# An adaptive feed-forward layer on one core: conditioning weights asked for ahead of x, and one x load and its maxima moved in the step before the second half

## The chip, the cores and the metric

The kernel runs on one core of one Trainium2 chip. Its metric is device time in microseconds, the lower the better. The kernel before was timed in three runs: 1572.83, 1573.0 and 1580.12 us, a median of 1573.0 us.

## The reference, cut to what matters

```python
x: (32, 128, 2048) f32       # batch, channel, time
w = weights[itok]            # one of 32 matrices (128 x 128) for each batch entry
c = einsum('bct,bcd->bdt', x, w)                       # conditioning
result = einsum('bnd,od->bno', c, W_base) + b_base     # W_base 2048 x 2048
logits = einsum('bnd,ed->bne', c, W_gate)              # 8 experts
route_w = top-2 of softmax(logits), normalised, as a one-hot sum
h = einsum('bnd,erd->bner', c, A)                      # rank 16 for each expert
delta = einsum('bner,eor->bno', h * route_w[..., None], B)
out = x + result + delta * SCALING
```

## The kernel before, in words

**Tiling.** The 32 batch entries go in 16 pairs. The contraction over 2048 time steps is cut into two halves of 1024. A step `n` (0 to 31, `NSTEP`) is one pair and one half: `pair(n)` gives pair `n % 16` and half `n // 16`. Steps 0 to 15 (`NP` is 16) use the first half of W_base, and store partial sums in `part_scratch`; steps 16 to 31 load these partial sums, add the second half and the low-rank delta, and store `out`. Float32 values are split into two float16 parts and scaled by powers of two, which is why the largest values of x and of the chosen conditioning matrix must be found before anything else is done with them.

**One step on TensorE.** `product(n, s, q)` (L1485) multiplies in a seven-product scheme (q from 0 to 6), for the two column halves `s`; a product is 12 matmuls of 128x512. Between them lie the conditioning of step n+1 (`cond`), `make_features(n)` (L1541, 48 matmuls into bank_h, which reads `FT`), `transpose_maxima(n+1)` (L1530), `spread_maxima(n+1)` (L1536, after product q=2) and in the second half `transpose_hw(n)` (L1574, after q=4). The order in the program is product(n,0,0), make_features(n), transpose_maxima(n+1), product q=1, product q=2, spread_maxima(n+1), q=3, q=4, transpose_hw(n).

**VectorE.** `find_maxima(n)` (L1007) waits for x and for both w_cond tiles, and reduces them: L1011 reads x, L1013 reads w_cond. `finish(n, s, c)` (L1059) turns a finished product into an output tile in `t_sums`: L1070 and L1075. There are eight tiles a step, numbered m = 8n + 4s + c; `t_sums` has two buffers, so tile m waits until GpSimd has added tile m-2. At the end of a step VectorE runs find_maxima(n+2), then finish of C12, C21 and C22 of s = 1. The next step begins with `find_top(n+1)` (L1016), `features(n)` (L1083) and, in the second half, `route_tokens` and `weigh_features` (L1103 to L1150).

**GpSimd.** `add_bias(m)` (L571, L574) waits for the loaded residual tile `x_res` m and adds the bias; `add_r(m)` (L594, L602) adds what `finish` made. In the first half the order is add_bias(m+1), then add_r(m).

**Queues.** SyncE issues nearly all DMAs, in an order written out by hand (L489 on). At j = 0 of a step it stores tile 8n, may store a piece of transformed W_base (`store_piece`, L408), stores h, calls `load_x(n+2)` (L380) once `xp_lo` says that the buffer X has been read, and then loads residual tile m+5. Step 15 has extra loads at j = 0: h0 and `FT`, the second half's feature weights. ScalarE copies product results (`copy_p`, L697) and issues, through its own DMA queue, the 14 loads of 1 MB that replace the weights TT in steps 15 and 16 (`load_weights`, L805, the issue is L812). For s = 1, q = 0 that load waits until the last pieces that store_piece wrote have landed, the last one being the store that step 15 issues just after its tile 120.

Of the kernel before, what the change touches and what calls it, by code (L numbers as in the profile page):

```python
# [9 lines left out]
NP = NB // 2  # L10
KH = T // 2
# [42 lines left out]
def adaln_ffn_kernel(nc, x, idx, w_cond, w_base, b_base, w_gate, a_lora, b_lora, out):  # L54
# [6 lines left out]
    with ExitStack() as ctx:  # L61
# [317 lines left out]
        def _(sp):  # L379
            def load_x(n):  # L380
                p, k = pair(n)
                sp.dma_start(X[:, :, :], x[2 * p:2 * p + 2, :, k * KH:(k + 1) * KH].rearrange("b p t -> p b t")
                             ).then_inc(x_in, 16)
                for i in range(2):
                    b = 2 * p + i
                    row = sp.value_load(idx_sb[0:1, b:b + 1], min_val=0, max_val=w_cond.shape[0] - 1)
                    sp.dma_start(WC[:, i, :], w_cond[bass.ds(row, 1)].rearrange("a c d -> c (a d)")
                                 ).then_inc(wc_in, 16)

            def load_rows(g):  # L390
                k, u = g // NU, g % NU
# [97 lines left out]
            for n in range(NSTEP):  # L489
                p, k = pair(n)  # L490
                g, chunks = window_of(n)
                if chunks:
                    if chunks[0] == 0:
                        store_inv(g)
                    store_piece(g, chunks[0], 0)
                    store_piece(g, chunks[0], 1)
                    store_piece(g, chunks[1], 0)
                    if len(chunks) > 2:
                        store_piece(g, chunks[1], 1)
                for j in range(4 if n == 0 else 0, 8):  # L500
                    m = 8 * n + j
                    store_tile(m)
                    if len(chunks) == 2 and j == 0:
                        store_piece(g, chunks[1], 1)
                    if n == NP - 1 and j == 0:
                        sp.wait_ge(bg_out[H0_PIECE], piece_turn(NU - 1, C4 - 2, 1))
                        sp.wait_ge(h_out, 16)
                        sp.dma_start(h0[:, :, :].rearrange("p b n -> p (b n)"), h_dram[0]).then_inc(h_in, 16)
                        sp.wait_ge(h_done, NP)
                        sp.wait_ge(ft_out, 16)  # L510
                        sp.dma_start(FT[:, :, :, :].rearrange("p f s n -> p (f s n)"), ft_dram).then_inc(ft_in, 16)
                    if len(chunks) > 2 and j == 0:
                        store_piece(g, chunks[2], 0)
                    if j == 0:
                        if k == 0:
                            sp.wait_ge(h_ready, n + 1)
                            sp.dma_start(h_dram[p], h[:, :, :].rearrange("p b n -> p (b n)")).then_inc(h_out, 16)
                        if n + 2 < NSTEP:
                            sp.wait_ge(xp_lo, 2 * (n + 2))
                            load_x(n + 2)  # L520
                        if k == 1 and n + 1 < NSTEP:
                            sp.wait_ge(h_ready, n + 1)
                            sp.dma_start(h0[:, :, :].rearrange("p b n -> p (b n)"), h_dram[p + 1]).then_inc(h_in, 16)
                    if len(chunks) > 2 and j == 0:
                        store_piece(g, chunks[2], 1)
                        store_piece(g, chunks[3], 0)
                    if len(chunks) > 2 and j == 1:
                        store_piece(g, chunks[3], 1)
                    if m > 0 and m - 1 + NXR < 8 * NSTEP:
                        last = m - 1  # L530
                        sp.wait_ge(xr_out[xr_slot(last)], xr_turn(last))
                        load_tile(last + NXR)
                    if n < len(WINDOWS) and j == (4 if n == 0 else 3):
                        sp.wait_ge(cond_done, 4 * (n + 2))
                        load_rows_ahead(*window_ahead(n))
                    if n == NP - 1 and j == 3:
                        sp.wait_ge(bg_inv_out, 16 * NU)
                        load_inv(0)
                    if n == NP - 1 and j == 6:
                        sp.wait_ge(bt_out, 16)  # L540
                        sp.dma_start(BT[:, :, :].rearrange("p s o -> p (s o)"), bt_dram).then_inc(bt_in, 16)
                if n == NP - 1:
                    load_inv(1)
# [451 lines left out]
        def _(dve):  # L995
# [11 lines left out]
            def find_maxima(n):  # L1007
                if n > 0:
                    dve.wait_ge(amax_tr, n)
                dve.wait_ge(x_in, 16 * (n + 1))  # L1010
                nc.vector.tensor_reduce(amax[:, 0:2], X[:, :, :], AX_X, ALU.max, apply_absolute_value=True)  # L1011
                dve.wait_ge(wc_in, 32 * (n + 1))
                nc.vector.tensor_reduce(amax[:, 2:4], WC[:, :, :], AX_X, ALU.max,  # L1013
                                        apply_absolute_value=True).then_inc(amax_ready, 1)
# [330 lines left out]
            for n in range(1, NSTEP):  # L1345
                more, second = n + 1 < NSTEP, n >= NP
                g, chunks = window_of(n)
                whole = len(chunks) > 2
                ahead, ahead_chunks = window_ahead(n)
                if chunks:  # L1350
                    add_up_first(g, chunks[0])
                if n <= NP:
                    find_top(n + 1)
                features(n)
                if n > NP and more:
                    find_top(n + 1)
                if second:
                    route_tokens(n)
                    weigh_features(n)
                if chunks:  # L1360
                    lower_chunk(g, chunks[0])
                finish(n, 0, C11)
                if more:
                    scale_x(n + 1)
                if whole:
                    lower_chunk(g, chunks[1])
                if second:
                    split_hwT_lo(n)
                if more:
                    split_x_lo(n + 1, 0)  # L1370
                    split_x_lo(n + 1, 1)
                if chunks and not whole:
                    lower_chunk(g, chunks[1])
                if whole:
                    lower_chunk(g, chunks[2])
                finish(n, 0, C12)
                if whole:
                    lower_chunk(g, chunks[3])
                if second:
                    add_delta(n, 0)  # L1380
                finish(n, 0, C21)
                finish(n, 0, C22)
                if second and more:
                    s_lower(n + 1, A11)
                if second:
                    add_delta(n, 1)
                if not second:
                    s_lower(n + 1, A11)
                    s_lower(n + 1, S1)
                    sum_s2(n + 1)  # L1390
                    s_lower(n + 1, A12)
                    finish(n, 1, C11)
                    s_lower(n + 1, S2)
                    sum_s4_s3(n + 1)
                    s_lower(n + 1, A22)
                    s_lower(n + 1, S4)
                    s_lower(n + 1, S3)
                else:
                    if more:
                        s_lower(n + 1, S1)  # L1400
                        sum_s2(n + 1)
                    add_delta(n, 2)
                    if more:
                        s_lower(n + 1, A12)
                    finish(n, 1, C11)
                    add_delta(n, 3)
                    if more:
                        s_lower(n + 1, S2)
                        sum_s4_s3(n + 1)
                        s_lower(n + 1, A22)  # L1410
                    add_delta(n, 4)
                    if more:
                        s_lower(n + 1, S4)
                        s_lower(n + 1, S3)
                    add_delta(n, 5)
                if ahead_chunks and ahead_chunks[0] == 0:
                    scales_ahead(ahead)
                if n + 2 < NSTEP:
                    find_maxima(n + 2)
                finish(n, 1, C12)  # L1420
                if second:
                    add_delta(n, 6)
                    add_delta(n, 7)
                finish(n, 1, C21)
                finish(n, 1, C22)
# [317 lines left out]
```

## Time and profile before

| What | Value |
|---|---|
| median of three runs | 1573.0 us (1572.83 to 1580.12) |
| the profiled execution's own time | 1578.86 us |
| its span, first to last instruction | 1577.0 us |
| TensorE (PE) busy | 1511.6 us, 96% |
| VectorE (DVE) busy | 1356.1 us, 86% |
| ScalarE (ACT) busy | 626.0 us, 40% |
| GpSimd (POOL) busy | 647.4 us, 41% |
| mean granted TensorE clock | 0.985 of full speed |
| mean DMA rate over the span | 150 GB/s |

Busy time is the time in which an engine executes; the span is what the engines are shares of. TensorE is busy nearly all the time, so only time in which it is idle, or runs at a lower clock, can be won without removing matmuls. Two stretches of the page's forty show it: the first few, where all engines wait for each other, and the two around the middle of the span, where the DMA rate is at its highest (246, 336 and 225 GB/s in three slices) and VectorE falls from 9 tenths to 6 and 7.

### The profile page before, as it was taken

To read this page: it belongs to the slowest core of one execution; us is meant where nothing else is said; L and a number is where in the kernel's file an instruction comes from. 1 tells how busy PE (TensorE), PEld (TensorE's weight loads), DVE (VectorE), ACT (ScalarE), POOL (GpSimd) and SP (SyncE) were. 2 spreads that over 40 slices of the span, in tenths; PEclk is the share of its full clock that TensorE was granted. 3 is DMA by queue.
4 is the path that set the end of the run, shared out by engine and by line. 5 is a ranking of instruction groups with operands and counts; after the bars stand their busy time and mean duration, and the time that the engine had idled before them with its cause. 6 is when DMAs were issued, how large, how long until landed. Compare 5 with 4: busy or idle time off the path is not lost.

```text
span 1577.0 us, 25816 instructions
## 1 busy us (share of the span) xinstructions
PE 1511.6 (96%) x9411; PEld 812.0 (51%) x9411; DVE 1356.1 (86%) x2257; ACT 626.0 (40%) x1026; POOL 647.4 (41%) x508
## 2 busy tenths in 40 slices
PE   5778999999899999999989999999999999999998
PEld 5554555555455555555535455555455555455553
DVE  5787999999899999999967888888888888888875
ACT  6854454444544445444413332223332323332321
POOL 2564656666666565665622122122122122122122
PEclk8899999999999999999999999999999999999999
DMA  6234556655565555665796343344433344433342
GB/s 232 94 132 150 159 168 179 191 158 157 153 184 170 165 162 178 179 187 153 246 336 225 107 125 100 98 141 128 114 121 96 105 141 123 117 117 91 117 111 74
DMA packets 169567, 235.95 MB, mean 150 GB/s; under 512 B 71898, under 2 KB 88794, under 8 KB 167130
## 3 DMA queue, kind: packets, MB, share of 16 engines
q1 hardware_dynamic: 167426, 219.63, 46.0%
q10 hardware_dynamic: 2016, 14.68, 2.4%
q8 instruction: 75, 1.23, 0.3%
q14 instruction: 50, 0.41, 0.1%
HBM read 147.83 MB, written 86.43 MB: 149 GB/s over the span
## 4 chain that ended last, share of the span: by engine, by line
PE 66%; DVE 17%; issue 4%; DMA 3%; POOL 2%; ACT 1%; SPq 0%; ACTq 0%; DVEq 0%; POOLq 0%
PE bank_x L1429 8%; PE bank_x L1431 8%; PE bank_x L1430 7%; PE bank_y L1429 7%; PE bank_y L1430 7%; PE bank_y L1431 7%; DVE t_sums L1070 3%; PE bank_z L1429 2%; PE bank_z L1431 2%; PE bank_z L1430 2%; DVE t_sums L1075 2%; PE bank_h L1430 2%; PE bank_h L1429 2%; PE bank_h L1431 2%; DVE s_parts L1045 2%
## 5 line engine op out<-in xcount | busy, mean ns | idle before, releaser
L602 POOL TENSOR_TENSOR x_res<-x_res,t_sums 128x512 f32<-128x512 f32 x255 | 353.5, 1388 | 837.6 <-DVE t_sums L1075 676.5
L1429 PE MATMUL bank_y<-TT,s_parts 128*128 128x512 f16 x768 | 294.6, 384 | 4.7 <-DVE TT L1185 4.2
L1430 PE MATMUL bank_y<-TT,s_parts 128*128 128x512 f16 x768 | 294.4, 383 | 0.0
L1431 PE MATMUL bank_y<-TT,s_parts 128*128 128x512 f16 x768 | 294.1, 383 | 0.0
L1429 PE MATMUL bank_x<-TT,s_parts 128*128 128x512 f16 x768 | 291.7, 380 | 1.6 <-DVE TT L1185 1.6
L1430 PE MATMUL bank_x<-TT,s_parts 128*128 128x512 f16 x768 | 291.1, 379 | 0.0
L1431 PE MATMUL bank_x<-TT,s_parts 128*128 128x512 f16 x768 | 291.1, 379 | 0.0
L710 ACT ACTIVATE p_copies<-bank_x,y_inv 128x512 f32<-128x512 f32 x128 | 87.7, 685 | 408.9 <-PE bank_x L1431 298.9
L1075 DVE TENSOR_TENSOR t_sums<-t_sums,inv_w 128x512 f32<-128x512 f32 x255 | 230.7, 905 | 8.7
L1045 DVE TENSOR_TENSOR s_parts<-a_full,s_parts 128x512 f16<-128x512 f32 x224 | 200.0, 909 | 33.6 <-ACT s_parts L695 33.6
L574 POOL TENSOR_TENSOR x_res<-x_res,BT 128x512 f32<-128x512 f32 x128 | 210.7, 1646 | 25.5 <-DMA x_res<-in_x_dram 24.2
L695 ACT ACTIVATE s_parts<-a_full 128x512 f16<-128x512 f32 x224 | 139.0, 628 | 145.8 <-DVE a_full L1050 61.1
L1431 PEld LDWEIGHTS bank_y<-TT,s_parts 128*128 128x128 f16 x768 | 75.9, 99 | 92.8 <-issue 3.9
L1431 PEld LDWEIGHTS bank_x<-TT,s_parts 128*128 128x128 f16 x768 | 75.2, 98 | 90.8 <-issue 0.3
L1429 PEld LDWEIGHTS bank_y<-TT,s_parts 128*128 128x128 f16 x768 | 75.8, 99 | 87.8 <-DVE TT L1185 4.7
L676 ACT ACTIVATE a_full<-bank_c 128x512 f32<-128x512 f32 x128 | 76.2, 595 | 112.6 <-PE bank_c L1431 112.6
L1070 DVE SCALAR_TENSOR_TENSOR t_sums<-bank_y,y_inv,p_copies 128x512 f32<-128x512 f32 x128 | 95.1, 743 | 28.4 <-PE bank_y L1431 28.4
L1429 PEld LDWEIGHTS bank_x<-TT,s_parts 128*128 128x128 f16 x768 | 75.1, 98 | 84.5 <-DVE TT L1185 1.5
L1430 PEld LDWEIGHTS bank_y<-TT,s_parts 128*128 128x128 f16 x768 | 75.8, 99 | 82.9 <-issue 2.8
L1430 PEld LDWEIGHTS bank_x<-TT,s_parts 128*128 128x128 f16 x768 | 75.2, 98 | 82.2 <-issue 0.3
L1070 DVE SCALAR_TENSOR_TENSOR t_sums<-bank_x,y_inv,p_copies 128x512 f32<-128x512 f32 x128 | 95.0, 743 | 10.6 <-PE bank_x L1431 6.7
L1429 PE MATMUL bank_c<-w_cond_parts,x_parts 128*128 128x128 f16 x512 | 93.0, 220 | 4.8 <-ACT a_full L676 2.6
(243 smaller groups left out, 2757.5 us busy)
## 6 DMA issues: line engine op xcount, KB each, us to landing
x<-in_x_dram SPq DMA_DIRECT2D x32, 1024.0 KB, 6.1
x_res<-in_x_dram SPq DMA_DIRECT2D x128, 256.0 KB, 4.2
part_scratch<-x_res SPq DMA_DIRECT2D x128, 256.0 KB, 3.6
x_res<-part_scratch SPq DMA_DIRECT2D x128, 256.0 KB, 3.9
out_dram<-x_res SPq DMA_DIRECT2D x128, 256.0 KB, 2.8
wt_scratch<-late_words SPq DMA_DIRECT2D x64, 224.0 KB, 3.4
TT<-wt_scratch ACTq DMA_DIRECT2D x14, 1024.0 KB, 7.7
x_parts<-in_L_ffn_W_base_dram SPq DMA_DIRECT2D x18, 512.0 KB, 6.6
```

The source lines that it names most:

```text
L574: link(nc.gpsimd.tensor_tensor(XR[:, xr_slot(m), :], XR[:, xr_slot(m), :], bias[:, o:o + Q], ALU.add))
L602: nc.gpsimd.tensor_tensor(XR[:, xr_slot(m), :], XR[:, xr_slot(m), :], TM[:, m % 2, :], ALU.add).then_inc(r_added, 1)
L676: nc.scalar.activation(AF[:, u, :], BC[:, :], ACT.Copy, scale=Y_DOWN).then_inc(af_copied, 1)
L695: nc.scalar.activation(SO[:, slot(n, q), 0, :, :], quads(AF[:, af_of[q], :]), ACT.Copy).then_inc(s_hi, 1)
L710: nc.scalar.activation(PC[:, at, :], src[:, :], ACT.Copy, scale=y_inv[:, par, row:row + 1]).then_inc(p_copied, 1)
L1045: nc.vector.tensor_tensor(SO[:, slot(n, q), 1, :, :], quads(AF[:, af_of[q], :]), SO[:, slot(n, q), 0, :, :], ALU.subtract).then_inc(s_lo, 1)
L1070: nc.vector.scalar_tensor_tensor(out=TM[:, m % 2, :], in0=src[:, :], scalar=y_inv[:, n % 2, c // 2:c // 2 + 1], in1=PC[:, at, :], op0=ALU. ...
L1075: nc.vector.tensor_tensor(TM[:, m % 2, :], TM[:, m % 2, :], inv_w[:, o:o + Q], ALU.mult).then_inc(r_ready, 1)
L1429: nc.tensor.matmul(dst, lhs[0], rhs[0], start=start, stop=False, skip_group_check=chained)
L1430: nc.tensor.matmul(dst, lhs[0], rhs[1], start=False, stop=False, skip_group_check=chained)
L1431: return nc.tensor.matmul(dst, lhs[1], rhs[0], start=False, stop=stop, skip_group_check=chained)
```

## The change

In `load_x` the two loads of w_cond (with the register loads that find their addresses) are issued ahead of the load of x, in all 32 steps. In step 15 alone, `load_x(17)` is issued right behind the store of tile 120, ahead of the weight piece, h0, `FT` and the store of h; and VectorE runs `find_maxima(17)` behind `finish(15, 1, C12)`, no longer ahead of it.

```diff
             def load_x(n):
                 p, k = pair(n)
-                sp.dma_start(X[:, :, :], x[2 * p:2 * p + 2, :, k * KH:(k + 1) * KH].rearrange("b p t -> p b t")
-                             ).then_inc(x_in, 16)
                 for i in range(2):
                     b = 2 * p + i
                     row = sp.value_load(idx_sb[0:1, b:b + 1], min_val=0, max_val=w_cond.shape[0] - 1)
                     sp.dma_start(WC[:, i, :], w_cond[bass.ds(row, 1)].rearrange("a c d -> c (a d)")
                                  ).then_inc(wc_in, 16)
+                sp.dma_start(X[:, :, :], x[2 * p:2 * p + 2, :, k * KH:(k + 1) * KH].rearrange("b p t -> p b t")
+                             ).then_inc(x_in, 16)
@@
                     store_tile(m)
+                    if n == NP - 1 and j == 0:
+                        sp.wait_ge(xp_lo, 2 * (n + 2))
+                        load_x(n + 2)
                     if len(chunks) == 2 and j == 0:
                         store_piece(g, chunks[1], 1)
                     if n == NP - 1 and j == 0:
@@
-                        if n + 2 < NSTEP:
+                        if n + 2 < NSTEP and n != NP - 1:
                             sp.wait_ge(xp_lo, 2 * (n + 2))
                             load_x(n + 2)
@@
-                if n + 2 < NSTEP:
+                if n + 2 < NSTEP and n != NP - 1:
                     find_maxima(n + 2)
                 finish(n, 1, C12)
+                if n == NP - 1:
+                    find_maxima(n + 2)
```

## Rows read from the trace of the kernel before

**Rows 1.** VectorE's waits in the whole span: for whom, us, times, longest.
```profile
DVE amax L1011 <- DMA x<-in_x_dram: 5.4, 1, 5.4
DVE amax L1013 <- DMA w_cond<-in_L_cond_weights_dram: 3.0, 1, 3.0
```

**Rows 2.** VectorE in time: start, duration, instruction, idle before and releaser.
```profile
801.65 2.29 DVE L1011 TENSOR_REDUCE amax<-x 128x2 f32<-128x2048 f32 x1 [5.45 <-DMA x<-in_x_dram]
806.92 0.42 DVE L1013 TENSOR_REDUCE amax<-w_cond 128x2 f32<-128x256 f32 x1 [2.98 <-DMA w_cond<-in_L_cond_weights_dram]
...
811.32 0.75 DVE L1070 SCALAR_TENSOR_TENSOR t_sums<-bank_x,y_inv,p_copies 128x512 f32<-128x512 f32 x1 [2.60 <-POOL x_res L602]
...
814.21 0.75 DVE L1070 SCALAR_TENSOR_TENSOR t_sums<-bank_x,y_inv,p_copies 128x512 f32<-128x512 f32 x1 [1.26 <-POOL x_res L602]
...
816.27 0.56 DVE L1022 TENSOR_SCALAR top_diag<-ident,top_pow 4x4 bf16<-4x4 f32 x1
```

**Rows 3.** TensorE in time, around its idle stretches.
```profile
802.41 0.22 PE L1429 MATMUL bank_h<-FT,s_parts 128*128 128x136 f16 x1
...
807.39 0.27 PE L1534 MATMUL bank_c<-ident,amax 128*4 128x128 f32 x1 [1.98 <-DVE amax L1013]
808.14 0.58 PE L1429 MATMUL bank_y<-TT,s_parts 128*128 128x512 f16 x1 [0.48 <-DVE t_sums L1070]
...
816.89 0.17 PE L1538 MATMUL bank_c<-top_diag,ones 4*128 4x4 bf16 x1 [1.76 <-DVE top_diag L1022]
...
825.90 0.69 PE L1579 MATMUL bank_d<-ident,late_words 128*128 128x128 f32 x2 [3.55 <-DVE late_words L1148]
```

**Rows 4.** One 10 us stretch: busy time by engine, granted clock, DMA share, GB/s.
```profile
825.00:835.00 10.00, 9.10 (x38) 4.16 (x39) 8.93 (x17) 4.30 (x7) 1.55 (x2) 0.66 1.02 395
```

**Rows 5.** GpSimd in time, from its long wait on.
```profile
808.52 1.32 POOL L574 TENSOR_TENSOR x_res<-x_res,BT 128x512 f32<-128x512 f32 x1 [19.63 <-DMA x_res<-in_x_dram]
...
812.49 1.59 POOL L602 TENSOR_TENSOR x_res<-x_res,t_sums 128x512 f32<-128x512 f32 x1
```

**Rows 6.** SyncE's DMA issues in time: start and how long the issue took.
```profile
771.96 6.26 SPq L442 DMA_DIRECT2D part_scratch<-x_res  x1
779.42 0.36 SPq L412 DMA_DIRECT2D wt_scratch<-late_words  x1
...
783.13 0.62 SPq L382 DMA_DIRECT2D x<-in_x_dram  x1
784.49 3.48 SPq L387 DMA_DIRECT2D w_cond<-in_L_cond_weights_dram  x2
788.01 3.74 SPq L429 DMA_DIRECT2D x_res<-in_x_dram  x1
```

**Rows 7.** The same issues: size, and us from issue to landing.
```profile
wt_scratch<-late_words SPq DMA_DIRECT2D x1, 224.0 KB, 15.6
FT<-ft_scratch SPq DMA_DIRECT2D x1, 816.0 KB, 15.4
x<-in_x_dram SPq DMA_DIRECT2D x1, 1024.0 KB, 18.4
x_res<-in_x_dram SPq DMA_DIRECT2D x1, 256.0 KB, 20.4
```

**Rows 8.** ScalarE and its DMA queue in time.
```profile
795.17 0.33 ACTq L812 DMA_DIRECT2D TT<-wt_scratch  x1
...
808.09 0.69 ACT L710 ACTIVATE p_copies<-bank_x,y_inv 128x512 f32<-128x512 f32 x1 [12.04 <-DVE t_sums L1070]
```

**Rows 9.** DMA queues (q1 SyncE, q10 ScalarE), 795 to 798 us: packets, MB, share.
```profile
q1 hardware_dynamic: 541, 1.21, 102.0%
q10 hardware_dynamic: 3, 0.01, 0.7%
```

**Rows 10.** The same, 798 to 808.4 us.
```profile
q10 hardware_dynamic: 429, 3.13, 71.5%
q1 hardware_dynamic: 588, 0.95, 24.1%
```

**Rows 11.** The first step: VectorE's first maxima, and TensorE's weight load for their transpose.
```profile
10.23 2.28 DVE L1011 TENSOR_REDUCE amax<-x 128x2 f32<-128x2048 f32 x1
...
16.81 0.09 PEld L1534 LDWEIGHTS bank_c<-ident,amax 128*4 128x4 f32 x1
```

## The prediction

> **What bounds the kernel now.** I read the shares of the page first: TensorE is busy for 1511.6 of 1577.0 us, so a change that removes no matmul can win only idle time of TensorE or time at a lower clock. Then the waits by engine: in the whole span VectorE waits for x once and for w_cond once, 5.4 and 3.0 us [rows 1]. VectorE in order of time shows that both are the same find_maxima, that of step 17, at 801.65 and 806.92 us [rows 2]. So the moved lines act at one place in 32 steps, and TensorE in order of time shows what that place costs [rows 3]. I count five losses:
>
> - idle from 805.41 (807.39 less 1.98) to 808.14, the 0.27 us transpose apart: 2.5 us, ended by the maxima and by finish C12 behind them
> - product q = 1 begins with matmuls of 0.58 to 0.63 us; eight stand 0.43 us apart instead of 0.22, which is 1.7 us
> - idle 1.76 us before 816.89, until VectorE has found the largest maximum (L1022)
> - idle 3.55 us before 825.90, until VectorE has weighed the features (L1148)
> - behind that, thirteen matmuls at 0.43 us: 2.8 us. The granted clock of this stretch is 0.66 [rows 4], a mix of the levels 1.2 and 2.4 GHz.
>
> All five are 12.3 us, 0.8% of the time. The question is how much of this hangs on x and w_cond.
>
> **A second chain lies beside the first.** After find_maxima VectorE waits twice for GpSimd (2.60 us before 811.32, 1.26 us before 814.21) [rows 2], because a t_sums buffer is free only when GpSimd has added the tile two before. GpSimd itself sat for 19.63 us until residual tile 125 had landed [rows 5]: issued at 788.01, 20.4 us to landing, so 808.4 us [rows 6, 7]. From there it is busy without a gap: add_bias(125), add_r(124), add_bias(126), and add_r(125) from 812.49 to 814.08 [rows 5]; that frees VectorE's last finish at 814.21, then come find_top (L1022 at 816.27) and 9 us of routing. So the third and fourth loss, and the clock behind them, follow from tile 125 as much as from x. Removing the wait for x alone would let TensorE start q = 1 at 805.4 instead of 808.14, run q = 1 and q = 2 (5.2 us), and wait longer for the same 816.89. The first two losses would only change places. **The forecast therefore hangs on when tile 125 lands, not on when x does.**
>
> **The change part by part.**
>
> *find_maxima(17) behind finish C12.* The same two reductions of 2.29 and 0.42 us [rows 2] run either way. The finish needs product q = 5 of s = 1, whose last matmul starts at about 797; it now ends near 799. x will be there (next paragraph), so the maxima end at 802, before TensorE asks for them at 805.4. The 2.5 us idle goes from here. The instructions add up to nothing. ScalarE's copy, which waited 12.04 us for this finish until 808.09 [rows 8], now runs at about 802.5, and the 1 MB weight load behind it in ScalarE's order is issued 5.6 us sooner. It queues behind three others and so can delay only what lands late.
>
> *load_x(17) issued sooner.* SyncE is held by the store of tile 120 until 778.22, and then has a gap to 779.42 [rows 6]. It now issues w_cond, w_cond and x from about 779.0 to 781.1; one register load costs 0.74 us (783.75 to 784.49) [rows 6]. Behind it are queued: the weight piece (779.42 before, now about 781.2), h0, FT, the store of h, and tile 125. The wait for xp_lo that is now ahead of all these was over at 776.7, so it costs nothing. The bytes ahead of tile 125 are the same. What changes is the order. x had landed at 783.13 + 18.4 = 801.5; ahead of the slow piece it should land by 795, in any case before 799.
>
> *Two transfers pay for that.* First the weight piece: landed 779.42 + 15.6 = 795.0, and 0.15 us later ScalarE issues the load that waits for it, the first of three weight loads of 1 MB [rows 7, 8]. With x and w_cond ahead (1.18 MB at some 400 GB/s, 3 us) it lands at about 798, and these three start 3 us later. They are needed 30 us on. Second FT: landed 781.84 + 15.4 = 797.2, 2.2 us after the piece, while ScalarE's queue moved only 0.01 MB [rows 7, 9]. The same 2.2 us after 798 is 800.2; TensorE asks for it at 802.41 [rows 3]. That cover is 2 us thin, and in the same stretch nothing is lost until make_features begins after 805: q = 1 started at 808.14 anyway.
>
> *Tile 125.* From 798 to 808.4 the two queues moved 429 packets of 7.3 KB (weights) and 588 of 1.6 KB on average [rows 10]. Per engine that is 27 and 37 in 10.4 us: nearly a packet of each in turn, so a small transfer of SyncE's queue pays about 0.3 us for each packet and engine while weights are in flight. Before, the rest of x, w_cond (512 B packets) and tile 125 all stood in this stretch. After, only the end of FT, h and tile 125 do: about 8 + 8 packets on each engine beside the weights, which start at about 798 + 2.1 = 800.2. That gives 800.2 + 0.8 (h alone) to + 6: I take 804.5, bounds 801 and 808.4 (no gain at all, if what is conserved is the sum of bytes).
>
> The Trainium skill ("DMA: Bandwidth & Descriptors", Queues, rings and completion order) says that each DMA engine goes round-robin between the queues it has work for, a packet at a time. Where this rule speaks against the change: while weights are in flight, which they are up to 795, the packets of w_cond and x that are put ahead would each wait for a weight packet, and the piece and FT behind them would land later than the 3 us by bytes; by 32 packets on an engine at 0.3 us it would be up to 9 us. That result is the third rival below, in rows of this case.
>
> *The sum for the transition.* With tile 125 at 804.5: add_bias to 805.8, add_r(124) to 807.1; tile 126 (809.7 before) at about 808, then add_bias(126) to 809.3, add_r(125) 1.6 us, last finish at 811.0 instead of 814.2. VectorE's chain and TensorE's two waits behind it come 3.2 us sooner: **minus 3.2 us**. The clock may give 2.8 us more if the idle before transpose_hw falls to the 1.76 us behind which no slow matmul stood [rows 3]; I don't count it.
>
> *w_cond ahead of x in the other 31 steps.* x is issued some 2 us later. It lands about 6 us after its issue there and is read 15 us on; no other find_maxima waited [rows 1]. Price zero, as long as that slack is there. In the first step x is needed at 10.23, and would come 2 us later; its maxima are used at 16.81 [rows 11], so that is hidden. But the loads behind x may slip by the bubble between two issues, and the start has no slack on ScalarE: 0 to 2 us, I take **plus 0.5 us** (nearest to zero, since the queue has 1 MB before it in transfer).
>
> Together -2.7 us: against the profiled span of 1577.0 it is 1574.3. The profiled execution took 1578.86 us, 5.9 us above the median of 1573.0; the difference carries over, so 1573.0 - 2.7 = 1570.3. With some weight on the clock's share I write **1570.0 us**.
>
> **The rivals.**
>
> 1. *Tile 125 as before.* Bytes and engines are full from 775 to 806, and FIFO order alone conserves when the last of them lands. TensorE's q = 1 starts sooner and waits longer at 816.89. For it: a DMA rate that is at its ceiling either way. Time 1573.0 + 0.5 = 1573.5.
> 2. *All five losses go.* If tile 125 lands by about 799, VectorE's last finish is at 805 and routing ends before TensorE has done q = 4 (816.1). -12.3 + 0.5: 1561. For it: the three weight loads start later and 1.2 MB of SyncE's queue can pass in 3 us [rows 9]. Against it: FT, h and the piece must pass first.
> 3. *FT becomes the wait (slower).* x's and w_cond's packets, put ahead among weight packets, push FT behind 802.41. It costs nothing up to 806.9: features take 3.0, transpose 0.3, the two products 5.2 and the clock 1.7, and 816.9 was the end before. With 0.3 us for each of some 32 packets FT lands at about 797.2 + 9 to 13: at 810 it is 3.1 us. Time 1573.0 + 3.1 + 0.5 = 1576.6.
> 4. The change does what it says on SyncE's queue, since nothing it waits for is late; I give no chance to its having no effect on find_maxima.
>
> **How the numbers follow.** Forecast 1570.0 (1566 to 1573): 0.50. Rival 1: 0.20. Rival 2, 1561 with 1559 to 1565: 0.15. Rival 3: 0.15, nearly all of it under 1581. The range reaches to rival 2's centre and to rival 3's: 1561 to 1577. Faster or slower counts from 0.5% (7.9 us), which is about what a measurement of this kernel can tell from no change: under 1565.1 lies rival 2 and a tail of the forecast with the clock, 0.17; over 1580.9 a tail of rival 3, 0.04; within it 0.79.
>
> **What would show it.** In the profile of the changed kernel: no wait of L1011 or L1013; find_maxima(17) ends before features do; the piece lands near 798 and the weight load waits with it; FT's landing against the first bank_h matmul of step 16; GpSimd's long wait for x_res ends about 804.5 (with the start's shift added) and not at 808.5; the idle before L1538 and L1579 ends 3 us sooner. It would be wrong if TensorE's wait moved to bank_h (rival 3), if GpSimd's wait ended where it did (rival 1), or if the idle before L1579 were gone (rival 2). A change of more than 2 us in the first 110 us would make the start's term wrong.

## The result, and the profile after

The changed kernel is slower: 1595.8 us as the median of four runs (1587.62 to 1598.68), a ratio of 1.0122 to the kernel before, interval 1.0064 to 1.0179. I had forecast 1570.0 with a range of 1561 to 1577, and gave 0.04 to slower (over 1580.9). The ratio is taken against the three runs of the kernel before that are given above, whose mean is 1575.3 us; a fourth run of it took 4081.78 us and is not counted. The profiled execution took 1587.62 us, with a span of 1585.8 us against 1577.0. Beside the experiments the kernel before had medians of 1576.0 to 1577.3 us (18 to 29 runs); every ratio below is against its runs on the same chip. A recorded ratio need not equal the quotient of the two medians; for the kernels below the two differ by up to 0.0017, so differences of 0.001 between ratios say nothing.

find_maxima starts once in each step and cuts the span into stretches that can be compared. The step named is its argument, and find_maxima(n) runs at the end of step n-2:

| Stretch between the starts of find_maxima | before | after | difference |
|---|---|---|---|
| start of the span to that of step 2 | 147.1 | 146.1 | -1.0 |
| step 2 to step 16 | 607.5 | 622.1 | **+14.6** |
| step 16 to step 18 (the transition) | 100.7 | 96.0 | **-4.7** |
| step 18 to the end | 721.7 | 721.7 | 0.0 |

So in these two profiles the part on which the forecast spent nearly all its working came out near what it said, and a part that it priced at zero took three times as much away. The row of windows (length, busy time of PE, PEld, DVE, ACT and POOL with counts, granted clock, DMA share, GB/s) of the second stretch, before:

```profile
147.10:754.64 607.54, 600.73 (x3837) 320.22 (x3836) 583.02 (x729) 278.18 (x444) 373.45 (x286) 1.00 0.56 169
```

and after:

```profile
146.05:768.13 622.08, 603.01 (x3842) 320.29 (x3841) 573.66 (x730) 279.17 (x442) 369.13 (x286) 1.00 0.54 164
```

TensorE's idle time in it rose from 6.8 to 19.1 us, which is 12.3 of the 14.6 us; 2.3 us more are busy time at the same work. The waits by engine (who for whom, us, times, longest), here of the whole span, say for whom. After:

```profile
PE bank_d L1565 <- DVE diag_inv L1230: 15.0, 8, 3.5
DVE row_clamped L1007 <- ACT late_words L770: 26.9, 8, 4.5
SPq L429 <- DMA part_scratch<-x_res: 124.2, 58, 6.6
```

Before:

```profile
PE bank_d L1560 <- DVE diag_inv L1227: 3.7, 3, 3.1
DVE row_clamped L1004 <- ACT late_words L767: 11.3, 8, 3.0
SPq L429 <- DMA part_scratch<-x_res: 77.3, 49, 14.9
```

To be read from the bottom: SyncE waits 47 us longer for its own stores of partial sums to land (L429 is the next load of a residual tile, which needs the buffer). VectorE waits 16 us longer for ScalarE's row sums of W_base, whose rows SyncE asks for behind those waits. TensorE waits 11 us longer for the scales that VectorE makes of the sums. The eight times are the steps that begin a new unit of W_base. Seven of them lie in the second stretch, and in it alone TensorE's wait went from 0.6 to 11.4 us, nearly all of its 12.3 us of idle time, VectorE's from 8.3 to 23.5 and SyncE's from 52.4 to 102.5. TensorE's longest wait, 3.1 of the 3.7 us before and 3.5 of the 15.0 after, stands ahead of that stretch.

In the second half of the span SyncE also waits longer for its stores, there those of `out` (42.0 us against 14.6), and the last stretch still takes 721.7 us in both: in these two traces a later landing costs something only where the rows of W_base stand behind it.

One such step shows how it begins. SyncE's issues in time, before; x_parts is where the rows of W_base go:

```profile
295.83 0.36 SPq L412 DMA_DIRECT2D wt_scratch<-late_words  x1
296.23 0.56 SPq L517 DMA_DIRECT2D h_scratch<-h  x1
296.84 0.45 SPq L382 DMA_DIRECT2D x<-in_x_dram  x1
298.66 1.48 SPq L387 DMA_DIRECT2D w_cond<-in_L_cond_weights_dram  x2
...
300.66 0.43 SPq L442 DMA_DIRECT2D part_scratch<-x_res  x1
...
304.60 0.33 SPq L429 DMA_DIRECT2D x_res<-in_x_dram  x1
...
306.50 0.93 SPq L403 DMA_DIRECT2D x_parts<-in_L_ffn_W_base_dram  x2
```

and after:

```profile
296.74 0.36 SPq L412 DMA_DIRECT2D wt_scratch<-late_words  x1
297.14 0.56 SPq L520 DMA_DIRECT2D h_scratch<-h  x1
299.17 1.49 SPq L385 DMA_DIRECT2D w_cond<-in_L_cond_weights_dram  x2
300.71 0.44 SPq L387 DMA_DIRECT2D x<-in_x_dram  x1
...
301.70 0.43 SPq L442 DMA_DIRECT2D part_scratch<-x_res  x1
...
308.95 0.33 SPq L429 DMA_DIRECT2D x_res<-in_x_dram  x1
...
311.20 1.42 SPq L403 DMA_DIRECT2D x_parts<-in_L_ffn_W_base_dram  x2
```

The first issue is 0.91 us later after, so 0.91 us is to be taken off each difference. x then leaves 3.0 us later: it now stands behind a register load (1.47 us, from the end of the issue at 297.14 to 299.17), a w_cond, a second register load and a second w_cond. The store is issued at the same place as before, but 1 MB of x now starts moving just ahead of it, where it had 3.8 us of start. Its landing frees the next load 3.4 us later (308.95), and the rows leave 3.8 us later (311.20). ScalarE had not waited for rows in this step before. After, it does, and VectorE and TensorE follow (start, duration, and in brackets the idle time before and its releaser):

```profile
318.06 1.06 ACT L770 ACTIVATE late_words<-x_parts 128x1024 f16<-128x1024 f32 x1 [3.19 <-DMA x_parts<-in_L_ffn_W_base_dram]
320.42 0.17 DVE L1007 TENSOR_SCALAR row_clamped<-row_sum 128x2 f32<-128x2 f32 x1 [4.47 <-ACT late_words L770]
321.64 0.28 PE L1565 MATMUL bank_d<-diag_inv,ones 128*128 128x128 bf16 x2 [2.60 <-DVE diag_inv L1230]
```

The transition after, in SyncE's order, then as sizes and landing times of the weight piece, FT, x and tile 125 (rows of before: [rows 6, 7]):

```profile
793.15 1.59 SPq L385 DMA_DIRECT2D w_cond<-in_L_cond_weights_dram  x2
794.79 0.50 SPq L387 DMA_DIRECT2D x<-in_x_dram  x1
795.34 0.56 SPq L412 DMA_DIRECT2D wt_scratch<-late_words  x1
796.00 8.84 SPq L511 DMA_DIRECT2D late_words<-h_scratch  x1
804.94 2.27 SPq L514 DMA_DIRECT2D FT<-ft_scratch  x1
...
807.94 0.65 SPq L429 DMA_DIRECT2D x_res<-in_x_dram  x1
```

```profile
wt_scratch<-late_words SPq DMA_DIRECT2D x1, 224.0 KB, 15.9
FT<-ft_scratch SPq DMA_DIRECT2D x1, 816.0 KB, 8.8
x<-in_x_dram SPq DMA_DIRECT2D x1, 1024.0 KB, 15.7
x_res<-in_x_dram SPq DMA_DIRECT2D x1, 256.0 KB, 6.8
```

The splitting of x, from which both traces can be measured, ended at 776.74 before and at 790.41 after, 13.67 us later. The other engines there, after:

```profile
812.67 2.28 DVE L1014 TENSOR_REDUCE amax<-x 128x2 f32<-128x2048 f32 x1
...
822.99 0.75 DVE L1073 SCALAR_TENSOR_TENSOR t_sums<-bank_x,y_inv,p_copies 128x512 f32<-128x512 f32 x1 [4.01 <-POOL x_res L605]
```

```profile
814.76 1.26 POOL L577 TENSOR_TENSOR x_res<-x_res,BT 128x512 f32<-128x512 f32 x1 [13.85 <-DMA x_res<-in_x_dram]
...
820.25 1.27 POOL L577 TENSOR_TENSOR x_res<-x_res,BT 128x512 f32<-128x512 f32 x1 [2.88 <-DMA x_res<-in_x_dram]
```

```profile
816.26 0.22 PE L1434 MATMUL bank_h<-FT,s_parts 128*128 128x136 f16 x1
...
825.32 0.17 PE L1543 MATMUL bank_c<-top_diag,ones 4*128 4x4 bf16 x1 [0.77 <-DVE top_diag L1025]
835.79 0.69 PE L1584 MATMUL bank_d<-ident,late_words 128*128 128x128 f32 x2 [5.01 <-DVE late_words L1151]
```

### The profile page after: what moved, and what is told of

Same layout as the page of the kernel before. It is cut to its first block, busy times and chain, and to the rows that moved or that the text cites. A ratio compares the mean times of both kernels' runs of the same rounds, so it can differ in the third digit from the quotient of the medians.

```text
span 1585.8 us, 25816 instructions
## 1 busy us (share of the span) xinstructions
PE 1505.7 (95%) x9411; PEld 807.2 (51%) x9411; DVE 1349.0 (85%) x2257; ACT 627.7 (40%) x1026; POOL 641.5 (40%) x508
## 4 chain that ended last, share of the span: by engine, by line
PE 65%; DVE 14%; DMA 6%; issue 3%; POOL 2%; SPq 1%; ACT 0%; DVEq 0%; ACTq 0%; POOLq 0%
PE bank_x L1434 8%; PE bank_x L1435 7%; PE bank_x L1436 7%; PE bank_y L1434 7%; PE bank_y L1435 7%; PE bank_y L1436 7%; DMA x_parts<-in_L_ffn_W_base_dram 3%; DMA part_scratch<-x_res 3%; PE bank_z L1435 2%; PE bank_z L1434 2%; PE bank_z L1436 2%; DVE t_sums L1078 2%; PE bank_h L1435 2%; PE bank_h L1436 2%; PE bank_h L1434 2%
## 5 line engine op out<-in xcount | busy, mean ns | idle before, releaser
L577 POOL TENSOR_TENSOR x_res<-x_res,BT 128x512 f32<-128x512 f32 x128 | 205.1, 1603 | 50.1 <-DMA x_res<-in_x_dram 45.9
L1048 DVE TENSOR_TENSOR s_parts<-a_full,s_parts 128x512 f16<-128x512 f32 x224 | 193.8, 881 | 33.0 <-ACT s_parts L698 33.0
L1073 DVE SCALAR_TENSOR_TENSOR t_sums<-bank_x,y_inv,p_copies 128x512 f32<-128x512 f32 x128 | 95.1, 743 | 14.2 <-PE bank_x L1436 8.0
```

Source lines behind the costliest of these rows:

```text
L577: link(nc.gpsimd.tensor_tensor(XR[:, xr_slot(m), :], XR[:, xr_slot(m), :], bias[:, o:o + Q], ALU.add))
L1048: nc.vector.tensor_tensor(SO[:, slot(n, q), 1, :, :], quads(AF[:, af_of[q], :]), SO[:, slot(n, q), 0, :, :], ALU.subtract).then_inc(s_lo, 1)
L1073: nc.vector.scalar_tensor_tensor(out=TM[:, m % 2, :], in0=src[:, :], scalar=y_inv[:, n % 2, c // 2:c // 2 + 1], in1=PC[:, at, :], op0=ALU. ...
```

## The experiments

Three theories stood at the start. A: x issued later leaves the queue empty for a while and delays all that SyncE does behind it. B: the order of the packets itself, w_cond in front and x directly ahead of the store. C: nothing of the edit.

**w_cond ahead of x, alone.** Step 15 is not touched.

```diff
 def load_x(n):
-    (load of x)
     for i in range(2): (register load, load of w_cond)
+    (load of x)
```

> Only w_cond ahead of x in load_x; step 15 as before. Between the maxima of step 2 and of step 16 the changed kernel took 13.5 us more than before and the middle 4.7 us less. Theory A (gap): two register loads, some 2 us, now pass before x is issued, so the DMA queue stands empty, x and all that SyncE issues behind it (the stores of two tiles, and the loads that wait for their landing, the rows of W_base last) come 3 to 4 us later, and the rows are too late for ScalarE's row sums: +13 us, ratio 1.008 to 1.009. Theory B (order of packets: x stands directly ahead of the stores, w_cond in front of x): the same +13 us here. Theory C (nothing of the edit, but the run or its memory placement): no difference, ratio 1.000.

Measured: 1.0103 (1.0083 to 1.0122), 1591.9 us. Its stretch from step 2 to 16 is 623.8 us, 16.3 more than before. This part alone makes the loss, and C falls. To my surprise its transition took 95.1 us, as short as the changed kernel's, without the moves that were meant for it.

**The moves of step 15, alone.** x stays ahead of w_cond. (Not shown: the same two calls are left out, for step 15, where they stood.)

```diff
+                    if n == NP - 1 and j == 0:
+                        sp.wait_ge(xp_lo, 2 * (n + 2))
+                        load_x(n + 2)
@@
                 finish(n, 1, C12)
+                if n == NP - 1:
+                    find_maxima(n + 2)
```

> Only the moves in step 15 (load_x(17) issued behind the store of tile 120, its maxima behind the first of the last finishings); x stays ahead of w_cond. Theories A and B: first half as before, the middle 4 to 5 us shorter, 0.997 (1568 if before is 1573). Theory C: longer by 9 to 13 us, as the changed kernel. The forecast on record for the middle alone was -3.2 us.

Measured: 1.0006 (0.9987 to 1.0025), no difference. In the profiled execution the transition took 96.7 us, 4.0 us less than before, and step 2 to 16 took 609.1. So one trace shows a shorter transition, and the timed runs don't show the 0.997 that was expected of it.

**Both register loads ahead of x, then x, then w_cond.**

```diff
 def load_x(n):
+    rows = [register load for i in range(2)]
     (load of x)
     for i in range(2):
-        (register load)
         (load of w_cond, by rows[i])
```

> x stays ahead of w_cond, but both register loads are made ahead of x's issue, so that x is issued about 2 us later and the stores behind at the same time as before. Theory A: the stores and all behind them land late, as with w_cond first: +8 to +13 us (1.005 to 1.008). Theory B: x is still ahead of w_cond, no loss from packets in front of it; 0 to +2 us.

Measured: 1.0069 (1.0046 to 1.0092). Here x is still ahead of w_cond, and two thirds of the loss are there: x leaves at 3.6 us behind the splitting of x, where it left at 2.0. B in its form "w_cond's packets in front of x" falls as the main cause; its other form, x too close ahead of the store, is left (2.0 us of start here, 3.5 before).

**w_cond ahead of x, but the registers loaded where SyncE waits anyway.** (Not shown: `load_x` now takes the loaded registers, and issues w_cond ahead of x.)

```diff
                     m = 8 * n + j
+                    if j == 0 and n + 2 < NSTEP:
+                        ahead_rows = rows_for(n + 2)
                     store_tile(m)
@@
-                            load_x(n + 2)
+                            load_x(n + 2, ahead_rows)
```

> w_cond ahead of x as in the change, but in the steps the register loads are made ahead of the store of tile 8n, where SyncE waits anyway; step 15 not moved. x is then issued only 0.8 us later than before and w_cond stands in front of it. Theory A: the loss is nearly gone, 0 to +3 us, perhaps below zero since SyncE has 2 us less to do behind x. Theory B: the loss stays, +10 to +13 us.

Measured: 1.0034 (1.0019 to 1.0049). A third of the loss is left, more than A said and less than B. x left 1.1 us later than before and the store 1.4 us sooner.

**The same registers early, x ahead of w_cond as before.**

> x ahead of w_cond as before, register loads ahead of the store of tile 8n, step 15 not moved. x is issued at the same time as before, w_cond and the stores behind 1.5 us sooner. Theory A: the first half is as before or up to 3 us shorter; 0.997 to 1.000. Theory B, as now left over (what counts is that the stores follow x closely, with no gap): the first half is longer, +4 to +8 us, since the gap from x to the store falls from 3.5 to 1.9 us, as with early registers and w_cond first, which measured 1.0034 (its gap 1.1 us).

Measured: 1.0020 (1.0000 to 1.0039). x leaves as before, and the first store behind it 1.5 us sooner (the second at 7.2 us behind the splitting, as before); the stretch from step 2 to 16 is 611.1 us, 3.5 more. That is just short of what was expected if the store follows x too closely, and well above a gain: less work on SyncE brought nothing. The step near 255 us shows one reason: the store now has x only 2.05 us ahead of it, takes 6.2 us to land in place of 4.3, and the rows leave 0.5 us later than before.

**With the moves of step 15.**

> The same with the moves of step 15. First half as in the kernel without them; the middle 4 us shorter in the profile, as e2_step15_only showed (96.7 against 100.7 us between the maxima of steps 16 and 18): 0.994 to 0.998.

Measured: 1.0026 (1.0013 to 1.0040), outside what was expected; the transition was 101.4 us. The waits of TensorE in it name a new one, for the low-rank weights that SyncE loads at the end of step 15:

```profile
PE bank_d L1441 <- DMA BT<-bt_scratch: 6.5, 1, 6.5
```

**What passes the loss on: the request for the rows.** w_cond ahead of x stays as in the first experiment, and the rows of W_base are asked for ahead of two waits for a store.

```diff
+                    if 0 < n < len(WINDOWS) and j == 2:
+                        sp.wait_ge(cond_done, 4 * (n + 2))
+                        load_rows_ahead(*window_ahead(n))
                     if m > 0 and m - 1 + NXR < 8 * NSTEP:
                         last = m - 1
@@
-                    if n < len(WINDOWS) and j == (4 if n == 0 else 3):
+                    if n == 0 and j == 4:
```

> w_cond ahead of x in load_x as in e1_order_only (measured 1.0103), step 15 not moved, and one more edit: in steps 1 to 14 the rows of W_base are asked for at j = 2, as soon as the conditioning is done (about 9 us behind the splitting of x), and no longer behind two waits for the landing of a store. Theory A1 (the loss passes through SyncE's order: x late, so the stores land late, so the request for the rows is late): the rows are issued at about +9.3 us instead of +14.6, and the loss goes: 0.997 to 1.003. Theory A2 (what costs is the late residual tiles at GpSimd, or the bytes of x themselves): the loss stays above 1.006.

Measured: 0.9992 (0.9981 to 1.0004). The whole loss of 1.0103 is gone, while x, the stores and the residual tiles are as late as they were: SyncE's waits for its stores are still there, TensorE's for the scales are back at their size before (in the stretch from step 2 to 16 it is 0.4 us, against 13.4 in the first experiment).

```profile
SPq L429 <- DMA part_scratch<-x_res: 125.8, 61, 12.8
...
PE bank_d L1563 <- DVE diag_inv L1230: 4.2, 3, 3.8
```

**The rows sooner in the kernel before.**

> The kernel before with the same edit for the rows alone: asked for at about +9.3 us instead of +11.5. Theory A1: some of its 11 us of waits for row sums on VectorE go, which TensorE shows as 3.7 us before bank_d: -2 to -4 us, 0.998; the loads of two residual tiles come behind 1 MB of rows and may take it back: +2 us at worst.

Measured: 0.9986 (0.9971 to 1.0000).

**The rows later in the kernel before**, with nothing else changed.

```diff
-                    if n < len(WINDOWS) and j == (4 if n == 0 else 3):
+                    if n < len(WINDOWS) and j == 4:
```

> The kernel before, x first and step 15 untouched, only the rows of W_base asked for at j = 4 in place of 3: about +16.3 us behind the splitting of x instead of +11.5. Theory A1: rows issued at +12.0, +12.7, +13.7 and +14.6 us measured 1.002, 1.0034, 1.0069 and 1.0103; with about 0.3% for each us this gives 1.013 to 1.018, with no w_cond moved at all. Rival (x's own lateness or the stores' costs by itself, not the rows): 1.000 to 1.003.

Measured: 1.0204 (1.0183 to 1.0226), 1608.9 us, above the 1.013 to 1.018 expected: a loss twice that of the order of w_cond and x, with w_cond and x untouched. The wait is the same one, larger:

```profile
PE bank_d L1560 <- DVE diag_inv L1227: 30.1, 8, 5.3
```

**Only the maxima moved.** find_maxima(17) behind the finish, the load of x where it was.

> The kernel before with find_maxima(17) behind the finish of C12, and x(17) asked for where it was. If the landing of residual tile 125 holds the chain (the forecast's theory), the finish comes sooner and VectorE still waits for GpSimd: the same time, 0.999 to 1.001, and TensorE's wait for the maxima stays (they need x at 801.5 us and w_cond at 806.9 in the trace of before). Rival: the order on VectorE alone brings the middle's 4 us: 0.997.

Measured: 1.0004 (0.9993 to 1.0015). The trace shows what the prediction said of a case in which only the wait for x goes: TensorE waited only 1.1 us for the maxima, started q = 1 sooner, and then sat waiting for the largest maximum:

```profile
PE bank_c L1540 <- DVE top_diag L1022: 5.7, 1, 5.7
```

GpSimd's wait for tile 125 was 20.0 us, as before.

**The changed kernel with the rows sooner.**

> The changed kernel (both parts) with the rows of W_base asked for at j = 2 in steps 1 to 14. By theory A1 the loss in the first half goes as it did for the order alone (1.0103 to 0.9992), and what is left is what the moves of step 15 are worth on top: the middle was 96.0 us in the profile of the changed kernel against 95.1 and 96.5 with the order alone, so nothing: 0.998 to 1.001. If the moves of step 15 are worth their own 4 us: 0.995 to 0.997.

Measured: 0.9996 (0.9979 to 1.0013). The loss is gone here too, and no gain from the moves shows.

**The moves of step 15 with the rows sooner**, x ahead of w_cond.

> x ahead of w_cond as before, the moves of step 15, and the rows asked for sooner. The rows sooner alone measured 0.9986, the moves of step 15 alone 1.0006. Sum of both: 0.999. If the middle's 4 us, seen in one profile of the moves alone, hold in the timed runs: 0.996 to 0.997.

Measured: 0.9982 (0.9967 to 0.9997), 1575.6 against 1576.4 us: the lowest ratio of this study, by a hair better than before, and 1.4% below the changed kernel's.

Set beside each other, the time follows when the rows are asked for, whatever made them late. Us behind the end of the splitting of x, in the step that starts near 255 us of each trace:

| Kernel | x issued | rows issued | ratio |
|---|---|---|---|
| rows sooner | 2.0 | 9.3 | 0.9986 |
| w_cond first, rows sooner | 4.7 | 9.3 | 0.9992 |
| before | 2.0 | 11.5 | 1 |
| early registers, x first | 2.0 | 12.0 | 1.0020 |
| early registers, w_cond first | 3.1 | 12.7 | 1.0034 |
| registers, x, w_cond | 3.6 | 13.7 | 1.0069 |
| w_cond first | 4.7 | 14.6 | 1.0103 |
| rows later | 2.0 | 16.8 | 1.0204 |

From 11.5 us on, each microsecond costs some 0.3 to 0.4%, 5 to 7 us over the eight steps (between neighbouring rows it is 0.2 to 0.45%); below, next to nothing. The quotients of the medians give the same order from "before" down. The second row and the last show that x's own issue time is not what counts.

## Why the prediction was wrong

**The step that failed** is "w_cond ahead of x in the other 31 steps ... Price zero". It was argued from who waits for x: no find_maxima waited [rows 1], and x has 15 us of slack. That no find_maxima waits was true and is still true after the change, where VectorE's list of waits has neither L1014 nor L1016. What I didn't follow is what is queued behind x on SyncE. x's delay reached nobody through x; it reached TensorE over five links: the landing of a store, the next load of a residual tile that waits for it, the rows of W_base behind that in SyncE's order, ScalarE's sums, VectorE's scales. Measured: +14.6 us in one profiled execution of the changed kernel, +1.03% or 16 us for the order alone in timed runs. The kernel before was already near the edge: VectorE had eight waits for these row sums, 11.3 us, and TensorE three behind them, 3.7 us (shown above), which a look at the list of waits would have named. How near, the later runs show: rows issued 1.2 us later already cost 0.34%. The queue behind a moved load was followed in step 15, and not in the 31 other steps.

**The size of the delay** was off too. I took x to be some 2 us later; it was 2.6 to 3.0 us. The register load of 0.74 us [rows 6] was read in step 15, behind x's own issue; between the issue ahead of it and the first w_cond it takes 1.1 us before and 1.2 after in the step near 255 us, and 1.4 and 1.5 us in the step near 296.

**The transition, by its terms.** Measured behind the end of the splitting of x (776.74 and 790.41), the changed kernel against the forecast: the weight piece landed at 20.8 us (forecast 21.3, before 18.3), FT at 23.3 (forecast 23.5, before 20.5), asked for at 25.9, so it was hidden as said. x landed at 20.1; "by 795" would have been 18.3, the bound of 799 held. Tile 125 landed at 24.3 (forecast 27.8, before 31.7), VectorE's last finish started at 32.6 (forecast 34.3, before 37.5). TensorE's transpose_hw started at 45.4 (before 49.2). The stretch became 4.7 us shorter; the forecast said 3.2, and it found them in another place. By its own list of five losses the 2.5 us of idle before q = 1 and the 1.7 us of slow matmuls in it are gone, 1.76 us became 0.77, 3.55 became 5.01, and the 2.8 us of slow matmuls behind that became 1.7 (eight at 0.43 us). Together that is 7.5 us in place of 12.3: 2.0 us less idle, and 2.8 us less at the lower clock, which I didn't count. VectorE's last finish came 4.9 us sooner, but the routing behind it took 1.1 us longer.

In this trace the mechanism was right in that a residual tile and not x holds the chain: the last finish waited 4.01 us for GpSimd. But it is tile 126 now. Its landing held GpSimd up to 820.25, 29.8 us behind the splitting (forecast 31.3). The maxima moved alone agree (GpSimd waits 20.0 us, TensorE 5.7 us at L1540, ratio 1.0004). And the landings came out on another course than the one forecast: SyncE stood for 8.84 us in the issue of the load of h0, so FT was issued at 14.5 us and tile 125 at 17.5 (before 5.1 and 11.3), and then took 8.8 and 6.8 us to land in place of 15.4 and 20.4. That the landing of FT fits to 0.2 us is in part luck.

**But no gain shows in timed runs.** Four pairs of kernels differ by the load of x(17) and its maxima alone: 1.0006 against 1, 1.0026 against 1.0020, 0.9996 against 0.9992, 0.9982 against 0.9986. All four differences are 0.0006 or less (in the last two pairs each ratio is against the runs of the kernel before on its own chip), and the first interval, 0.9987 to 1.0025, leaves out the 0.9980 that 3.2 us would be. In the profiles the transition takes 96.0, 96.7, 100.0, 101.0 and 101.4 us with the moves, and 95.1, 96.5, 96.7, 98.1, 98.9, 99.1, 100.7, 100.7 and 100.8 without them (98.1 with the maxima alone). So one profile of before (100.7) stood at the long end of a spread, and the 4.7 us are within it.

The spread may not be all chance, though. Of the nine without the moves, the three with w_cond ahead of x took 95.1, 96.5 and 96.7 us, the six with x ahead 98.1 to 100.8. In those three the maxima of step 17 wait for x alone (2.2, 3.8 and 5.3 us) and no longer for w_cond, which before landed 3.0 us too late behind x. The shorter transition of the changed kernel may thus belong to the order of w_cond and x as much as to the moves. One profile of each kernel can't settle it, and in timed runs it doesn't show either (rows sooner: 0.9992 with w_cond first, 0.9986 with x first).

One thing that takes the gain back is seen: in three of the five kernels with the moves TensorE then waits for BT, 4.7, 2.2 and 6.5 us, a load that SyncE issues at j = 6 of step 15 (in one of the nine others 3.3 us). Whether that makes up for all the moves bring is open.

**The start.** The 0.5 us that I added there don't show: step 2's maxima begin at 146.1 after and 147.1 before, and between 144.4 and 148.2 in all kernels.

**The rivals.** None was it. Rival 3 (FT) was to be slower by pushing packets ahead among the weights; by its 32 packets at 0.3 us, which was worked out beside the round-robin rule of the Trainium skill ("DMA: Bandwidth & Descriptors", Queues, rings and completion order), the piece would have come 9 us later. It came 2.5 us later [rows 6, 7], about what the bytes say. (The cover of FT in rival 3 adds up to 10.2 us, not 10.0, and ended at 806.7; that changes nothing.) The slower side needed a rival in the first half, with the rows of W_base as its place, and there was none. The 0.04 given to slower had nothing to do with the loss that came.

## What to carry to other kernels

When a load is moved later by a microsecond or two, its own reader's slack is only the first question; the second is the list of everything behind it on the issuing queue, and above all a wait for a landing there, since it turns the delay of bytes into a delay of issue for all that follows. Look in the list of waits for small entries on the critical engine (3.7 us here) and for the repeated ones of the engine it waits for (eight here, 11.3 us): they show which chain has little slack left, and such a chain is the first to pay. And where a stretch differs by a few microseconds between two single profiles, compare the stretch over more kernels before you call it a gain.

## What the runs showed of the hardware

A 1 MB load issued shortly ahead of a 256 KB store delays the store's landing, the more the closer it is. In the step near 255 us the first store behind x took 4.3 us, counted to the issue of the load that waits for its landing, in the kernel before, where x had 3.5 us of start; 6.5 and 6.2 us with 2.0 and 2.05 us of start (both register loads first; early registers, x first); and 7.1 us after, with 1.0. Less work on the issuing engine was no gain by itself: with the registers loaded early and the first store issued 1.5 us sooner behind x, the ratio was 1.0020.
